# Context attention: the last norm in three pieces, with maxima between them

## The chip, the cores and the metric

The kernel runs on one core of a Trainium2 chip. The metric is the device time of one execution in microseconds (us), lower is better. Times are medians of several executions; a profile is one further execution, with every engine's instructions recorded. The engines are TensorE (PE, its weight loads shown apart as PEld), VectorE (DVE), ScalarE (ACT), GpSimd (POOL) and SyncE (SP), which here issues the DMAs.

## What is computed

Six layers follow each other on a tensor x of 8 batches, 512 tokens and 256 features; each is added to its input and normalised. The change touches the second, attention to a context:

```
wq = (q @ wq_w.T + wq_b).reshape(b, t, H, DH)          # H = 16 heads of DH = 16
wk = (k @ wk_w.T + wk_b).reshape(b, t, H, DH)
wv = (v @ wv_w.T + wv_b).reshape(b, t, H, DH)
scores = einsum('bthd,bshd->bhts', wq, wk) / sqrt(DH)
probs  = softmax(scores, axis=-1)
attn   = einsum('bhts,bshd->bthd', probs, wv).reshape(b, t, d)
...
x = _layernorm(x + (attn @ wo_w.T + wo_b))             # over the 256 features, eps 1e-5
```

Inputs and outputs are float32. The layers before it (gated linear attention) and behind it (mixture of experts, Mamba, a second attention, a gated feed-forward) are not changed.

## The kernel before

The kernel is one program in which each layer is a stage with its own buffers; a barrier stands between stages. In a stage, every engine gets its own list of instructions and runs it in order; semaphores order the engines among each other. The function of this stage is `xattn_layer`.

**Steps.** A batch has 4 quads of 4 heads, a quad 8 steps, so a batch has 32 steps and the stage 256, with a run-in and a tail. At step u, TensorE computes the scores of two heads for 128 queries, with queries as rows (`by_queries(u)`, line 734), and VectorE takes their row maxima (`maxima(u)`, line 950, one reduction of 128x1024). Sixteen steps later (`LEAD`) the same scores are made again with keys as rows and the maximum subtracted through an extra row of the operands (`by_keys(u - 16)`, line 723); ScalarE takes their exponentials (line 887), and every second step `values` multiplies these with the values (line 752). Once in 8 steps there are transposes of the maxima (line 760) and of the finished heads (line 767); VectorE then divides the heads by their sums (`normalised`, lines 959 and 965, at steps 3, 11, 19 and 27 of the 32).

**Work of a batch at fixed steps.** `starts(u, i)` is true at step i (modulo 32) for the batch that comes next, `ends(u, i)` for the one just finished. For the next batch: transposes of x at step 14, key projection at 17, query projection at 20, value projection at 28 (`token_major`, line 131, 16 matmuls of 128x256). For the finished one: transposes of its attention at 23, output projection at 25 (`OUT`; line 131 again). Within a step, TensorE's order is keys, values, queries, then transposes and projections.

**The norm.** At step 25, behind that step's maximum, VectorE waits for the output projection, adds it to x (line 1010) and runs the whole norm (`Norm.vector`): `moments` are 4 statistics (line 155), 4 aggregations (line 159) and a copy of the variance (line 169); GpSimd turns that into the reciprocal root (`Norm.gpsimd`, lines 186 and 188); `apply` waits for it and normalises x in place (line 178, 4 instructions). At step 31 SyncE waits for `x_out` and stores x.

**Regions.** All blocks of scores and projections are written to three regions of PSUM (`region`), taken in turn by `claim`. A claim makes TensorE wait until the block three claims earlier has been read: a block of keys by ScalarE's exponential, a block of queries by VectorE's maximum, the output projection by the addition, a value projection by ScalarE's copy. In the order of the claims around the norm these are: keys 26, queries 26, keys 27, queries 27, keys 28, queries 28, value projection, keys 29, queries 29, keys 30 (named by step). The output projection is claimed between queries 25 and keys 26. So keys 27 wait for the addition, keys 28 for maximum 26, the value projection for maximum 27, queries 29 for maximum 28.

The steps at which the last batches end: batch 6 ends inside the loop, but no value projection follows it, since there is no batch 8; batch 7 ends in the tail, where there are no maxima.

Of the kernel before, what the change touches and what calls it, by code (L numbers as in the profile page):

```python
# [41 lines left out]
def flat(v):  # L42
    return v.rearrange("p a n -> p (a n)")
# [7 lines left out]
def times(v, n):  # L51

    return v.unsqueeze(1).to_broadcast([v.shape[0], n, v.shape[1]])


def counter():

    return iter(range(1, 1 << 20)).__next__
# [603 lines left out]
def xattn_layer(nc, A, K, psum, x_in, x_out, weights, SLOTS):  # L662
# [3 lines left out]
    with ExitStack() as ctx:  # L666
        st = Stage(nc, ctx, "xattn", psum, K["sems"], {"short": psum[0:REGIONS], "pv": [psum[REGIONS][:, 0, :]],
                                                       "rows": [psum[REGIONS][:, 1, :]]})
        ident = K["ident"]
        wq, wk, wv, wo = (weights[n] for n in ("xwq", "xwk", "xwv", "xwo"))  # L670
        XS, RING, STEPS, LEAD = 3, 5, 2 * NT, 16
        EL, QUADS = STEPS * XQ, B * XQ
        LAST = B * EL
        xs = [st.sb(f"x{i}", [NT, D]) for i in range(XS)]
# [11 lines left out]
        norm = Norm(st, 0)  # L686
# [10 lines left out]
        def quad(u):  # L697
            return u // STEPS, u % STEPS // 2, u % 2


        def starts(u, i):
            return u // EL + 1 if u % EL == i and u // EL + 1 < B else None

        def ends(u, i):
            return u // EL - 1 if u % EL == i and 0 <= u // EL - 1 < B else None

        XT, KEYS, QUERIES, VALUES = 14, 17, 20, 28
        ATTN, OUT = 23, 25
        steps = range(-EL, LAST + EL)

        with nc.Block() as block:
# [228 lines left out]
            @block.vector  # L940
            def _(dve):
                V = nc.vector
                nth = counter()

                def maxima(u):
                    n, t, a = quad(u)
                    dve.wait_ge(*st.full(f"q{u}"))
                    if n >= 2 and u % STEPS == 0:
                        dve.wait_ge(*st.full(f"top{n - 2}"))
                    V.tensor_reduce(tops[:, n % 2, t, a::2], st.region(f"q{u}")[:], AX, ALU.max).then_inc(  # L950
                        st.emptying(f"q{u}"), 1)

                def normalised(n):
                    b, qd = divmod(n, XQ)
                    dve.wait_ge(*st.full(f"o{n}"))
                    heads = st.region(f"o{n}").rearrange("p (t h d) -> p t h d", t=NT, h=4)
                    if n:
                        dve.wait_ge(*st.emptied(f"o{n - 1}"))
                    V.reciprocal(recip[:], heads[:, :, :, 16]).then_inc(st.sem("dve_step"), 1)
                    dve.wait_ge(st.sem("dve_step"), nth())  # L960
                    if b and qd == 0:
                        dve.wait_ge(*st.full(f"attnT{b - 1}"))
                    for a in range(2):
                        at = 128 * a + 32 * qd
                        last = V.tensor_tensor(attn[:, :, at:at + 32].rearrange("p t (r d) -> p t r d", r=2),
                                               heads[:, :, 2 * a:2 * a + 2, 0:16],
                                               recip[:, :, 2 * a:2 * a + 2].unsqueeze(3).to_broadcast([P, NT, 2, 16]),
                                               ALU.mult)
                    last.then_inc(st.emptying(f"o{n}"), 1)

                def low(name, hi, lo, bias, b, count):
                    dve.wait_ge(st.sem("high"), count)
                    o = st.region(f"{name}{b}")
                    for c in range(DC):
                        last = V.scalar_tensor_tensor(lo[:, c, :], o[:, c, :], bias[:, c:c + 1],
                                                      hi[:, c, :].bitcast(F32), ALU.add, ALU.subtract)
                    last.then_inc(st.emptying(f"{name}{b}"), 1)

                V.tensor_scalar(q_bias[:], K["xwq_b"], 0.25, None, ALU.mult)
                weights.arrive(dve)  # L980
                V.tensor_scalar(wq[:], wq[:], 0.25, None, ALU.mult).then_inc(st.sem("wq_scaled"), 1)
                V.tensor_scalar(row[0:1, :], K["chunk_mask"][0:1, :], 0.0, 1.0, ALU.mult, ALU.add).then_inc(
                    st.sem("row"), 1)
                for c in range(DC):
                    last = V.tensor_scalar(v_bias[:, c, :], K["ones"][:], K["xwv_b"][:, c:c + 1], None, ALU.mult)
                last.then_inc(st.sem("v_bias"), 1)
                for va in vas:
                    V.memset(va[:, :, :, 17:32], 0.0)
                    last = V.memset(va[:, :, :, 16:17], 1.0)
                last.then_inc(st.sem("va_ones"), 1)  # L990
                for u in steps:
                    v = u - LEAD
                    if 0 <= u < LAST:
                        maxima(u)
                    if v >= 11 and v % STEPS == 3 and v // STEPS - 1 < QUADS:
                        normalised(v // STEPS - 1)
                    if (b := starts(u, KEYS)) is not None:
                        low("kp", khi, klo, K["xwk_b"], b, 2 * b + 1)
                    if (b := starts(u, QUERIES)) is not None:
                        low("qp", qhi, qlo, q_bias, b, 2 * b + 2)  # L1000
                    if starts(u, VALUES) == 0:
                        dve.wait_ge(*st.full("bias_rows"))
                        V.tensor_tensor(out_bias[:], st.region("bias_rows")[:, 0:D], K["xwo_b"], ALU.add).then_inc(
                            st.emptying("bias_rows"), 1)
                    if (b := ends(u, OUT)) is not None:
                        x = xs[b % XS]
                        dve.wait_ge(*st.full(f"out{b}"))
                        dve.wait_ge(st.sem("biased"), b + 1)
                        o = st.region(f"out{b}")
                        V.tensor_tensor(flat(x[:]), flat(x[:]), flat(o[:]), ALU.add).then_inc(st.emptying(f"out{b}"), 1)  # L1010
                        dve.wait_ge(*st.emptied(f"out{b}"))
                        norm.vector(dve, nth, x, x, "x_out")

            @block.gpsimd
            def _(pool):
                nth = counter()
                for u in steps:
                    if (b := starts(u, XT)) is not None:
                        x = xs[b % XS]
                        pool.wait_ge(*st.full(f"xT{b}"))  # L1020
                        pool.wait_ge(*st.emptied("bias_rows"))
                        nc.gpsimd.tensor_tensor(x[:], x[:], times(out_bias[:], NT), ALU.add).then_inc(
                            st.sem("biased"), 1)
                    if ends(u, OUT) is not None:
                        norm.gpsimd(pool, nth, K["neg_half"], 1e-5)
        st.zero_sems()

# [1699 lines left out]
```

## Time and profile before

| | us |
|---|---|
| median of 3 runs | 3092.56 (3082.69 to 3092.64) |
| profiled execution | 3089.96 |
| its span, first to last instruction | 3088.2 |
| TensorE busy in the span | 2559.2 (83%) |
| VectorE busy | 1638.7 (53%) |
| ScalarE busy | 1385.4 (45%) |
| GpSimd busy | 319.5 (10%) |
| mean granted TensorE clock | 0.901 of full |

Full clock is 2.4 GHz; the profile shows two levels, 1.0 and 0.5 (1.2 GHz). The context attention fills about 690 to 1356 us of the span. Additions of the output projection (line 1010) start at 843.7 us for batch 0, at 1158.09 for batch 4 and at 1345.9 for batch 7. In the bracket at the end of a row, "idle before <-releaser" is the time for which the engine stood still ahead of that instruction and what ended it.

### The profile page before, as it was taken

The numbers are of one execution on the slowest core, as the hardware profiler recorded it, in microseconds if no ns is written. First come the engines' busy times: TensorE is split into PE (matmuls) and PEld (weight loads), VectorE is DVE, ScalarE is ACT, GpSimd is POOL, SyncE is SP. The second block draws the span as 40 slices with busy tenths as digits, with TensorE's granted clock in tenths as the row PEclk, the third lists the DMA queues.
The fourth block names the chain that finished last, engine by engine and source line by source line (L and its number), as shares of the span: only waits on it lengthen the run. The fifth ranks groups of instructions, "written<-read, shape, count | busy, mean of one in ns | idle before, by whom it ended". The sixth has DMA issues, their size and how long they took to land. (4 is left out here: it accounts for less than half of the span.)

```text
span 3088.2 us, 31620 instructions
## 1 busy us (share of the span) xinstructions
PE 2559.2 (83%) x11456; PEld 1500.5 (49%) x11456; DVE 1638.7 (53%) x3416; ACT 1385.4 (45%) x1989; POOL 319.5 (10%) x299
## 2 busy tenths in 40 slices
PE   5888888857888888879998588887588888887998
PEld 3555655543333333355455355555344444444555
DVE  5665555525566666615443487878455555541222
ACT  2333333313555555532221565654277777772221
POOL 0110010000000000000166100000121111000000
PEclk8999888867999999978799799998789999998999
DMA  2000000005333333240035411111300000001000
GB/s 71 14 14 14 14 8 14 7 26 143 54 61 61 61 62 56 46 148 1 26 65 78 132 66 45 69 55 42 100 7 28 28 28 28 21 14 62 14 21 21
DMA packets 113394, 140.81 MB, mean 46 GB/s; under 512 B 22004, under 2 KB 96004, under 8 KB 113240
## 3 DMA queue, kind: packets, MB, share of 16 engines
q1 hardware_dynamic: 98888, 123.97, 14.8%
q0 software_dynamic: 11904, 14.69, 2.9%
q8 instruction: 92, 1.51, 0.2%
q14 instruction: 62, 0.51, 0.1%
q10 hardware_dynamic: 2448, 0.14, 0.1%
HBM read 77.89 MB, written 35.39 MB: 37 GB/s over the span
## 5 line engine op out<-in xcount | busy, mean ns | idle before, releaser
L950 DVE TENSOR_REDUCE xattn_tops<-region 128x2 f32<-128x1024 f32 x256 | 305.6, 1219 | 148.2 <-PE region L734 148.1
L887 ACT ACTIVATE xattn_probs<-region 128x1024 f32<-128x1024 f32 x256 | 256.2, 1022 | 154.1 <-PE region L723 153.2
L2085 PE MATMUL region<-psi_fT 128*128 128x512 f32 x512 | 247.3, 622 | 24.7 <-DVE psi_low L2361 15.2
L122 PE MATMUL region<-gla_xT,weights_even 128*128 128x512 f32 (+1 forms) x416 | 207.6, 652 | 31.3 <-ACT gla_xT L214 31.3
L723 PE MATMUL region<-xattn_qs,xattn_ks 49*128 49x512 f32 x512 | 126.6, 496 | 85.0 <-DVE xattn_tops L950 54.5
L122 PE MATMUL region<-mamba_xT,weights_odd 128*128 128x512 f32 x320 | 158.5, 644 | 3.2 <-DVE mamba_xh L1924 3.2
L2085 PEld LDWEIGHTS region<-psi_fT 128*128 128x128 f32 x512 | 93.8, 196 | 135.2 <-issue 101.9
L122 PEld LDWEIGHTS region<-gla_xT,weights_even 128*128 128x128 f32 (+1 forms) x416 | 78.0, 196 | 146.4 <-issue 110.7
L752 PE MATMUL region<-xattn_probs,xattn_va 128*32 128x512 f32 x1024 | 144.7, 633 | 1.3 <-ACT xattn_o_T L914 1.3
L131 PE MATMUL region<-weights_even,gla_work 128*128 128x256 f32 x512 | 123.5, 403 | 26.0 <-ACT gla_work L484 24.7
L734 PE MATMUL region<-xattn_ks,xattn_qs 48*128 48x512 f32 x512 | 126.5, 492 | 14.1 <-DMA xattn_ks<-xattn_khi 9.8
L2215 ACT ACTIVATE psi_wedge<-region 128x512 f32<-128x512 f32 x128 | 76.2, 595 | 117.3 <-PE region L2085 114.7
L723 PEld LDWEIGHTS region<-xattn_qs,xattn_ks 49*128 49x128 f32 x512 | 48.9, 190 | 163.5 <-DVE xattn_tops L950 95.3
L131 PEld LDWEIGHTS region<-weights_even,gla_work 128*128 128x128 f32 x512 | 103.2, 203 | 48.6 <-ACT gla_work L484 28.3
L1140 PE MATMUL region<-moe_xT,weights_even 128*128 128x512 f32 x256 | 126.7, 644 | 0.0
L734 PEld LDWEIGHTS region<-xattn_ks,xattn_qs 48*128 48x128 f32 x512 | 52.4, 201 | 135.7 <-issue 81.8
L2510 ACT ACTIVATE ffn_silu<-region 128x512 f32<-128x512 f32 x48 | 28.7, 597 | 187.3 <-PE region L2467 187.3
L471 ACT ACTIVATE gla_work<-region 128x1024 f32<-128x1024 f32 x8 | 8.2, 1024 | 220.4 <-PE region L378 220.4
L122 PEld LDWEIGHTS region<-mamba_xT,weights_odd 128*128 128x128 f32 x320 | 65.2, 209 | 85.8 <-issue 79.3
L2218 ACT ACTIVATE psi_wedge<-psi_wedge,psi_g_eps,psi_g_sq 128x512 f32<-128x512 f32 x128 | 104.1, 813 | 4.1
L2533 DVE TENSOR_TENSOR ffn_h<-ffn_silu,region 128x512 f32<-128x512 f32 x48 | 33.0, 687 | 131.1 <-ACT ffn_silu L2510 131.1
L2361 DVE CUSTOM_DVE_ANT_0 weights_even<-psi_wedge,region,psi_unsign 128x512 f32<-128x512 f32 x64 | 47.5, 746 | 86.8 <-ACT psi_wedge L2218 86.0
(501 smaller groups left out, 5226.2 us busy)
## 6 DMA issues: line engine op xcount, KB each, us to landing
weights_even<-mamba_cs SPq DMA_DIRECT2D x32, 512.0 KB, 4.6
xattn_qs<-xattn_qhi SPq DMA_DIRECT2D x128, 64.0 KB, 2.3
xattn_ks<-xattn_khi SPq DMA_DIRECT2D x128, 64.0 KB, 2.3
moe_sums<-moe_picked SPq DMA_DIRECT2D x9, 512.0 KB, 8.7
gla_x<-in_x SPq DMA_DIRECT2D x8, 512.0 KB, 3.8
x_after_gla<-gla_res SPq DMA_DIRECT2D x8, 512.0 KB, 2.9
xattn_x<-x_after_gla SPq DMA_DIRECT2D x8, 512.0 KB, 4.1
xattn_ctxT<-in_ctxT SPq DMA_DIRECT2D x8, 512.0 KB, 4.4
```

Source lines behind the costliest of these rows:

```text
L122: last = st.nc.tensor.matmul(o[0:m, i, :], w[:, c, col + i * P:col + i * P + m], rhs[:, c, :], start=c == 0, stop=c == kc - 1)
L131: last = st.nc.tensor.matmul(o[:, t * D:t * D + D], lhs[:, base + c, t * P:t * P + P], w[:, base + c, :], start=c == 0, stop=c == kc - 1)
L723: last = mm(o[:, r, :], ks[rows, ring(n), a, j * P:j * P + P], qs[rows, ring(n), a, :], start=True, stop=True)
L734: last = mm(o[:, r, :], qs[rows, ring(n), a, t * P:t * P + P], ks[rows, ring(n), a, :], start=True, stop=True)
L752: last = mm(o[32 * g:32 * g + 32, :], vas[b % 2][:, j, 2 * qd + r + 8 * a, :], probs[:, p % 3, a, r, :], start=j == 0, stop=j == NT - 1)
L887: A_(probs[:, p % 3, a, :, :], st.region(f"k{v}")[:], ACT.Exp).then_inc(st.emptying(f"k{v}"), 1)
L950: V.tensor_reduce(tops[:, n % 2, t, a::2], st.region(f"q{u}")[:], AX, ALU.max).then_inc(st.emptying(f"q{u}"), 1)
L1140: last = mm(o[:, a, :], w[:, c, (NE + i) * P:(NE + i) * P + P], xT[:, b, c, :], start=c == 0, stop=c == DC - 1)
L2085: last = mm(o[:, a, :], fT[:, h, 0, t * P:t * P + P], fT[:, h, 1 + a, :], start=True, stop=True)
L2215: A_(wedge[:, i % 2, :], st.region(f"s{b}_{i}")[:, 0, :], ACT.Relu).then_inc(st.sem("wedge_in"), 1)
L2218: A_(wedge[:, i % 2, :], wedge[:, i % 2, :], ACT.Sqrt, scale=g_sq[:], bias=g_eps[:]).then_inc(st.sem("wedge_root"), 1)
L2361: V.tensor_tensor_reduce(scores[b % 2][:, j, :], wedge[:, j % 2, :], st.region(f"s{b}_{j}")[:, 1, :], unsign[:], 1e30, ALU.add, ALU.min, l ...
```

## The change

The addition stays at step 25. The statistics move to step 26, behind that step's maximum, and the application to step 27, behind that step's maximum and the division of the heads. GpSimd's part of the norm moves to step 26 in its list. SyncE's list, the store at step 31 among it, is as it was. `moments` and `apply` are the two calls of which `Norm.vector` consists.

```diff
--- before.py
+++ after.py
@@ -1008,8 +1008,11 @@
                         dve.wait_ge(st.sem("biased"), b + 1)
                         o = st.region(f"out{b}")
                         V.tensor_tensor(flat(x[:]), flat(x[:]), flat(o[:]), ALU.add).then_inc(st.emptying(f"out{b}"), 1)
+                    if (b := ends(u, OUT + 1)) is not None:
                         dve.wait_ge(*st.emptied(f"out{b}"))
-                        norm.vector(dve, nth, x, x, "x_out")
+                        norm.moments(dve, nth, xs[b % XS])
+                    if (b := ends(u, OUT + 2)) is not None:
+                        norm.apply(dve, xs[b % XS], xs[b % XS]).then_inc(st.sem("x_out"), 1)
 
             @block.gpsimd
             def _(pool):
@@ -1021,7 +1024,7 @@
                         pool.wait_ge(*st.emptied("bias_rows"))
                         nc.gpsimd.tensor_tensor(x[:], x[:], times(out_bias[:], NT), ALU.add).then_inc(
                             st.sem("biased"), 1)
-                    if ends(u, OUT) is not None:
+                    if ends(u, OUT + 1) is not None:
                         norm.gpsimd(pool, nth, K["neg_half"], 1e-5)
         st.zero_sems()
```

## Rows read from the trace of the kernel before

**Rows 1.** The page, part 1: busy time, share of the span, instructions.
```profile
PE 2559.2 (83%) x11456; PEld 1500.5 (49%) x11456; DVE 1638.7 (53%) x3416; ACT 1385.4 (45%) x1989; POOL 319.5 (10%) x299
```

**Rows 2.** The page, part 5: line, engine, operation, count, busy and mean, idle before.
```profile
L950 DVE TENSOR_REDUCE xattn_tops<-region 128x2 f32<-128x1024 f32 x256 | 305.6, 1219 | 148.2 <-PE region L734 148.1
...
L723 PE MATMUL region<-xattn_qs,xattn_ks 49*128 49x512 f32 x512 | 126.6, 496 | 85.0 <-DVE xattn_tops L950 54.5
```

**Rows 3.** View of waits, 700 to 1376 us: who waited for whom, us, times, longest.
```profile
DVE xattn_x L178 <- POOL xattn_rstd L188: 11.8, 8, 1.5
```

**Rows 4.** Timeline of VectorE, batch 4: start us, us, line, [idle before <-releaser].
```profile
1158.09 1.22 DVE L1010 TENSOR_TENSOR xattn_x<-xattn_x,region 128x1024 f32<-128x1024 f32 x1 [2.75 <-PE region L131]
1159.34 1.41 DVE L155 BATCH_NORM_STATS2 xattn_stats<-xattn_x 128x6 f32<-128x256 f32 x4
...
1161.19 0.17 DVE L169 COPY xattn_var<-xattn_mv 128x4 f32<-128x4 f32 x1
1162.84 1.38 DVE L178 TENSOR_SCALAR xattn_x<-xattn_x,xattn_mv,xattn_rstd 128x256 f32<-128x256 f32 x4 [1.47 <-POOL xattn_rstd L188]
1164.13 2.35 DVE L950 TENSOR_REDUCE xattn_tops<-region 128x2 f32<-128x1024 f32 x2
```

**Rows 5.** Timeline of TensorE's matmuls beside it.
```profile
1158.32 0.40 PE L734 MATMUL region<-xattn_ks,xattn_qs 48*128 48x512 f32 x2
1159.36 0.50 PE L723 MATMUL region<-xattn_qs,xattn_ks 49*128 49x512 f32 x2 [0.64 <-DVE xattn_x L1010]
...
1161.22 0.66 PE L767 MATMUL region<-ident,xattn_o_T 128*128 128x128 f32 x4
1165.40 0.79 PE L723 MATMUL region<-xattn_qs,xattn_ks 49*128 49x512 f32 x2 [3.53 <-DVE xattn_tops L950]
...
1166.56 5.59 PE L131 MATMUL region<-weights_odd,xattn_ctxT 128*128 128x256 f32 x16
1172.07 0.50 PE L723 MATMUL region<-xattn_qs,xattn_ks 49*128 49x512 f32 x2
```

**Rows 6.** Windows of 1 us beside it; the third figure from the end is the clock.
```profile
1163.10:1164.10 1.00, 0.00 (x0) 0.00 (x0) 1.00 (x4) 0.00 (x0) 0.00 (x0) 0.72 0.66 103
...
1170.10:1171.10 1.00, 1.00 (x5) 0.88 (x4) 0.00 (x0) 0.00 (x0) 0.00 (x0) 0.87 0.00 0
```

**Rows 7.** Timeline of matmuls, batch 1, which has no norm at its step 25.
```profile
758.36 0.50 PE L723 MATMUL region<-xattn_qs,xattn_ks 49*128 49x512 f32 x2 [0.95 <-DVE xattn_qlo L975]
...
759.49 0.49 PE L723 MATMUL region<-xattn_qs,xattn_ks 49*128 49x512 f32 x2 [0.39 <-DVE xattn_tops L950]
...
761.58 0.63 PE L723 MATMUL region<-xattn_qs,xattn_ks 49*128 49x512 f32 x2
...
771.40 3.72 PE L131 MATMUL region<-weights_odd,xattn_ctxT 128*128 128x256 f32 x16
```

**Rows 8.** Timeline of all engines: GpSimd's bias addition beside two maxima.
```profile
1202.52 2.37 POOL L1022 TENSOR_TENSOR xattn_x<-xattn_x,xattn_out_bias 128x1024 f32<-128x1024 f32 x1 [39.72 <-PE region L114]
...
1204.33 2.35 DVE L950 TENSOR_REDUCE xattn_tops<-region 128x2 f32<-128x1024 f32 x2 [1.98 <-PE region L734]
```

**Rows 9.** Timeline, batch 6: addition, and the next blocks of line 723.
```profile
1302.78 1.22 DVE L1010 TENSOR_TENSOR xattn_x<-xattn_x,region 128x1024 f32<-128x1024 f32 x1 [2.75 <-PE region L131]
...
1310.10 0.63 PE L723 MATMUL region<-xattn_qs,xattn_ks 49*128 49x512 f32 x2 [3.53 <-DVE xattn_tops L950]
```

**Rows 10.** Windows of 1 us beside rows 7, columns as in rows 6.
```profile
759.00:760.00 1.00, 0.61 (x8) 0.28 (x10) 1.00 (x2) 0.93 (x1) 0.00 (x0) 1.00 0.39 53
760.00:761.00 1.00, 1.00 (x10) 0.09 (x10) 0.56 (x1) 0.98 (x1) 0.00 (x0) 0.88 0.65 103
```

**Rows 11.** Windows from the value projection's end to the output projection's, same columns.
```profile
775.00:843.60 68.60, 60.36 (x313) 24.55 (x312) 39.19 (x42) 38.42 (x47) 2.38 (x1) 0.90 0.29 50
...
1172.10:1236.50 64.40, 55.89 (x313) 22.50 (x312) 39.11 (x42) 38.35 (x47) 2.37 (x1) 0.97 0.26 46
```

## The prediction

> **What bounds the kernel now.** I read the page's busy times first: TensorE is busy 83% of the span and no other engine above 53% [rows 1], so what counts is where TensorE stands still. The edit touches the context-attention stage alone (about 690 to 1356 us). There the costliest groups are the row maxima on VectorE, 256 of 1219 ns, and the score matmuls of line 723, before which TensorE sat idle 85.0 us, 54.5 us of that for a maximum on VectorE [rows 2]. The view of waits has the one wait that the change is about: the last norm's application waited 11.8 us, 8 times, for GpSimd's reciprocal root [rows 3]. That sum is too small to be the point; what matters is who waits behind it.
>
> So I laid the two timelines of one batch beside each other, batch 4 of 0 to 7, whose output projection ends at 1158 us. Steps are counted modulo 32: the norm is at step 25, and TensorE's next blocks are keys and queries of steps 26 to 28, then the value projection (16 matmuls) at step 28. On VectorE: addition at 1158.09, statistics from 1159.34, their last copy ends at 1161.36, a stand until 1162.84, application until 1164.13, and only then the maxima of steps 26 and 27, together 2.35 us [rows 4]. On TensorE: step 27's work ends at 1161.88, then 3.53 us of idle, until the maximum of step 26 gives back a region; step 28's two blocks; the value projection at 1166.56, when the maximum of step 27 is ready; step 29 at 1172.07 [rows 5]. TensorE waits for VectorE here, and VectorE for the norm. The wait is on the path, since nothing else of TensorE can pass it: its queue is in order and the three regions are shared in turn.
>
> The clock falls in the same place. It goes to half its level at about 1163.5, while TensorE stands, and is back at about 1170.2 [rows 6]. So the value projection takes 5.59 us here [rows 5], where the same 16 matmuls took 3.72 us for batch 1, with no norm ahead of them [rows 7].
>
> **The change, part by part.** No instruction is added or removed: per batch the same 1 addition, 4+4+1 statistics, 2 on GpSimd and 4 applications are issued. The order on VectorE becomes addition, maximum 26, statistics, maximum 27, normalisation of the heads (step 27), application, maximum 28.
>
> *Addition.* Unmoved; it gives back the projection's region at the same moment, so keys of step 27 still start at 1159.36 [rows 5]. Zero.
>
> *Maximum 26 ahead of the statistics.* Its scores (1158.32 + 0.40) are ready before the addition ends at 1159.31 [rows 4, 5], so it runs at once, 1159.34 to about 1160.52 (half of 2.35). TensorE then doesn't wait for it at all: keys of step 28 can follow at 1161.88.
>
> *Statistics.* Their 2.02 us (1159.34 to 1161.36) [rows 4] now lie at 1160.55 to 1162.57. What is queued behind them is maximum 27, and behind that the value projection. Maximum 27 ends at 1162.6 + 1.2 = 1163.8, so the value projection starts at about 1163.88. Counted from the addition, that is 5.79 us, where it was 1166.56 - 1158.09 = 8.47: a gain of **2.68 us**. It is the stand of 1.48, the application of 1.29 and some gaps, less one start-up. TensorE itself would be there at about 1162.7 (1161.88 plus 0.8 for two blocks), so the wait is not gone: 1.2 us of it is left.
>
> *GpSimd.* Moved by one step, with nothing of its own queue between. Its 1.48 us (the stand) end at about 1164.1. The normalisation, 0.7 us after maximum 27, reaches 1164.5; the application finds the root ready with some 0.4 us to spare. The trace has no root beside a maximum. Its nearest row: a GpSimd addition of 2.37 us beside maxima of 2.35 us for two, neither longer than elsewhere [rows 8]. I take zero; the upper bound is a full maximum more, 1.2 us.
>
> *Application at step 27.* Ends at about 1165.8, maximum 28 at 1167.0. Cover: the value projection, busy to at least 1167.4; the first block that needs maximum 28 is the queries of step 29, over 1 us after that. So zero, and with GpSimd's upper bound still zero. Without the cover it would be the 1.29 us of the application. The store is issued six steps after step 25 and waits for the application only, as before.
>
> *Number of times.* Batches 0 to 5 have this form: 6 x 2.68 = 16.1 us. Batch 6 has no value projection behind it, only the 3.53 us of idle and then key blocks that need maxima 27, 28 and 29 [rows 9]; by the same arithmetic the block behind maximum 29 comes 2.7 us earlier. Batch 7 is the tail: no maxima are left, zero. Sum of the waits: **18.8 us**.
>
> *The clock.* This is the term without a row. Upper bound: with 1.2 us of idle in place of 3.53 the clock stays up and the projection takes 3.6 to 3.7 us, 6 x 1.9 = 11.4 us more. Lower bound: it falls anyway and lies on the projection, about 0.2 us each. Against the upper one speaks the trace: at 758 and 759 us TensorE was idle for only 0.95 and 0.39 us, and at about 760.4 the clock fell [rows 7, 10]. What the change leaves is 0.64 us ahead of keys of step 27 and 1.2 us ahead of the projection, close to that. In the plain loop it stays up through single waits of 0.5 to 0.9 us. I take the middle, 0.9 us each, **5.4 us**.
>
> The page "TensorE: Matmul & The Clock Gate" of the Trainium skill, section "HAM oscillation — how this bites in real kernels", ties the fall to single idle gaps longer than any that I expect here. By it the clock would stay up; the rows at 758 us speak against it as a sufficient rule. The sum by that page would be the rival "clock stays up" below.
>
> **Sum.** 16.1 + 2.7 + 5.4 = 24.2 us. The profiled execution took 3089.96 us (span 3088.2), so 3089.96 - 24.2 = **3065.8 us**. The median of the runs shown is 3092.56, 2.6 above it, their spread 10 us; I forecast by the profiled one. A gain of under 0.5% (15.5 us, about what a measurement of this kernel can tell) counts as no change.
>
> **The rivals.**
> *Clock stays up everywhere at the projection.* For it: the idle left is a third. Against it: the fall at 760.4. 18.8 + 11.4 = 30.2 us, 3059.8 us; with a low stretch less at the key projection, down to 3052. Chance 0.22.
>
> *The gain is paid back by low clock elsewhere in the batch.* Each batch becomes shorter, so the waits at the key and query projections (2.1 and 0.95 us) fall differently against the clock. What that is worth shows between the value projection and the next output projection: batch 0 to 1 took 68.6 us at a mean clock of 0.90, a later one 64.4 us at 0.97, with 313 matmuls each [rows 11]. That is 4.2 us. In three of six batches, with the projection's clock at its lower bound: 18.8 + 1.2 - 12.6 = 7.4 us, 3082.6; in one: 3074. Chance of this kind 0.21 (0.12 for a result still more than 15.5 us below).
>
> *Another wait takes over.* Maximum 27 is the new last wait, and only GpSimd's stand leaves the path, 7 x 1.48 = 10.4 us: 3079.6. For it: maximum 27 is indeed last. Against: the application has also left the way to it, by the order of the queue. The same result if the stage's pace were set by something slower than this chain, such as the stacking DMAs. Chance 0.05.
>
> *Slower.* One mechanism: the low clock as in batch 1 in all of batches 1 to 6, price 6 x 4.2 = 25.2 against 18.8 + 1.2 = 20.0: 3095. It decides from the fifth such batch on (5 x 4.2 = 21.0). Beyond 0.5% it would have to reach later stages too. Chance 0.03.
>
> *It doesn't do what it says.* The order of a queue is that of the code, so it does. Below 0.01.
>
> **How the numbers follow.** Forecast 0.48 (3060 to 3072), clock up 0.22, paid back 0.21, another wait 0.05, slower 0.03 (0.01 of it beyond 0.5%), rest 0.01. Below 3077: 0.48 + 0.22 + 0.12 = 0.82. Within 0.5%: 0.16. Above: 0.02. The range must hold 8 in 10: down to 3052 for a clock that stays up at the key projection too, up to 3079 for one or two batches paid back.
>
> **What would show it.** In the changed kernel's timeline a maximum stands between addition and statistics, and VectorE's stand for GpSimd (11.8 us) falls to the tail's 1.5. The value projection starts 5.8 us after the addition; idle ahead of line 723 for maxima falls from 54.5 by some 25 us, and some 7 us of idle appear ahead of the value projection. Its duration and the clock beside it settle the clock term: 3.7 us or 5.3. Addition to addition, 78.6 us now, becomes 74 to 75.5. Wrong would be: a projection that starts later than 5.8 us after the addition, queries of step 29 waiting for maximum 28, or a period above 76 with low clock at the key or query projection.

## The result

| | median us | runs | ratio to before (95%) |
|---|---|---|---|
| kernel before | 3092.60 (3082.69 to 3094.03) | 4 | |
| changed kernel | 3057.78 (3053.16 to 3060.05) | 4 | 0.9893 [0.9873, 0.9914] |

The change makes the kernel 1.1% faster, 34.8 us by the medians. The forecast was 3065.8 us in a range of 3052 to 3079. The profiled execution took 3060.05 us, its span is 3058.3 us, 29.9 us less than before. Seven executions of 3463 us and more, three of them of the kernel before, are left out of all medians below.

The page of the changed kernel has the two groups of [rows 2] as follows (line, engine, operation, count, busy and mean, idle before):

```profile
L950 DVE TENSOR_REDUCE xattn_tops<-region 128x2 f32<-128x1024 f32 x256 | 306.3, 1220 | 126.0 <-PE region L734 125.9
...
L723 PE MATMUL region<-xattn_qs,xattn_ks 49*128 49x512 f32 x512 | 126.4, 495 | 61.8 <-DVE xattn_tops L950 31.4
```

Idle time ahead of line 723 went from 85.0 to 61.8 us, all of it in waits for a maximum (54.5 to 31.4). The view of waits for the stage has a new wait, ahead of the value projections, and GpSimd's root is waited for only in the tail, where [rows 3] had it 8 times:

```profile
PE region L723 <- DVE xattn_tops L950: 31.4, 47, 1.2
...
PE region L131 <- DVE xattn_tops L950: 6.1, 6, 1.0
...
DVE xattn_x L178 <- POOL xattn_rstd L188: 1.5, 1, 1.5
```

Batch 4 again, VectorE's timeline, to be held against [rows 4]:

```profile
1145.62 1.22 DVE L1010 TENSOR_TENSOR xattn_x<-xattn_x,region 128x1024 f32<-128x1024 f32 x1 [2.76 <-PE region L131]
1146.76 1.22 DVE L950 TENSOR_REDUCE xattn_tops<-region 128x2 f32<-128x1024 f32 x1
1147.89 1.40 DVE L155 BATCH_NORM_STATS2 xattn_stats<-xattn_x 128x6 f32<-128x256 f32 x4
...
1149.73 0.17 DVE L169 COPY xattn_var<-xattn_mv 128x4 f32<-128x4 f32 x1
1149.81 1.22 DVE L950 TENSOR_REDUCE xattn_tops<-region 128x2 f32<-128x1024 f32 x1
...
1151.63 1.38 DVE L178 TENSOR_SCALAR xattn_x<-xattn_x,xattn_mv,xattn_rstd 128x256 f32<-128x256 f32 x4
1152.93 1.22 DVE L950 TENSOR_REDUCE xattn_tops<-region 128x2 f32<-128x1024 f32 x1
```

And TensorE's matmuls beside it, to be held against [rows 5]:

```profile
1149.67 0.39 PE L734 MATMUL region<-xattn_ks,xattn_qs 48*128 48x512 f32 x2
1151.08 3.72 PE L131 MATMUL region<-weights_odd,xattn_ctxT 128*128 128x256 f32 x16 [1.03 <-DVE xattn_tops L950]
1154.73 0.51 PE L723 MATMUL region<-xattn_qs,xattn_ks 49*128 49x512 f32 x2
...
1156.17 0.50 PE L734 MATMUL region<-xattn_ks,xattn_qs 48*128 48x512 f32 x2
```

VectorE doesn't stand still between the addition and the end of maximum 28. The value projection starts 1151.08 - 1145.62 = 5.46 us after the addition, where it was 8.47, after 1.03 us of idle, where there were 3.53 ahead of the keys of step 28; and it takes 3.72 us. Six of six are like this.

**Where the 29.9 us of the two profiles lie.** Four stretches, cut at the first key projection, the first addition and the last addition:

| stretch | before | after | |
|---|---|---|---|
| start to first key projection | 696.3 | 704.0 | +7.7 |
| to the addition of batch 0 | 147.5 | 141.0 | -6.4 |
| to the addition of batch 7 | 502.2 | 481.7 | -20.5 |
| to the end of the span | 1742.3 | 1731.6 | -10.7 |

Only in the third does an instruction stand at another place of its queue: in the fourth, batch 7's norm has no maxima beside it, and its order is as before. In the nine profiles of this study without added instructions the fourth lay between 1727.9 and 1742.3 us, and the first, which no edit touches, between 695.0 and 704.0. So a pair of profiles can't be read to better than some 14 us there, and the experiments below are read by the third stretch, from addition to addition, first and by the timed runs second.

From one addition to the next: 78.6, 78.6, 78.5, 78.5, 78.5, 66.2, 43.1 us before, 75.3, 75.3, 77.8, 72.3, 79.4, 61.3, 40.4 after. The waits (3.01) and the projection at full clock (about 1.9) make 4.92 us per batch, so one expects 73.7 in the first five. The sixth, 66.2 - 61.3 = 4.9, has just that, and the last one 2.7. The first five have in sum 11.8 us less gain than 5 x 4.92. Split by blocks, these five gained 3.1 us between key and query projection, lost 8.2 at the query projections, and lost 6.7 between them and the next addition, nearly all in the third and the fifth. That is the clock, at another place, as the timeline between the additions of batches 4 and 5 shows:

```profile
1196.97 0.50 PE L723 MATMUL region<-xattn_qs,xattn_ks 49*128 49x512 f32 x2 [2.13 <-DVE xattn_klo L975]
...
1201.23 5.73 PE L122 MATMUL region<-xattn_xT,weights_odd 128*128 128x512 f32 x8
...
1209.76 0.50 PE L723 MATMUL region<-xattn_qs,xattn_ks 49*128 49x512 f32 x2 [0.94 <-DVE xattn_qlo L975]
...
1210.89 0.50 PE L723 MATMUL region<-xattn_qs,xattn_ks 49*128 49x512 f32 x2 [0.39 <-DVE xattn_tops L950]
...
1213.12 1.97 PE L114 MATMUL region<-ident,xattn_attn 128*128 128x128 f32 x8
...
1216.93 1.93 PE L752 MATMUL region<-xattn_probs,xattn_va 128*32 128x512 f32 x8
```

The windows around the first fall (third figure from the end: granted clock) put it at about 1198.5 us, 1.5 us after TensorE resumed work behind the wait of 2.13 us:

```profile
1197.00:1198.00 1.00, 1.00 (x10) 0.31 (x10) 1.00 (x1) 0.49 (x1) 0.00 (x0) 1.00 0.00 0
1198.00:1199.00 1.00, 1.00 (x10) 0.20 (x2) 0.04 (x1) 0.53 (x1) 0.00 (x0) 0.76 0.00 0
1199.00:1200.00 1.00, 1.00 (x6) 0.71 (x4) 0.86 (x1) 0.00 (x0) 0.00 (x0) 0.50 0.00 0
```

The query projection takes 5.73 us here and 5.6 to 5.95 in three other batches; in five of the kernel before it took 3.70. The waits of 2.13, 0.94 and 0.39 us stood there before as well; only the clock answers to them otherwise. In the kernel before it was low from 1214.7 to 1218.2 us, behind the same key projection, and was back before the query projection began at 1218.96; here it is low from 1198.5 to 1205.3, mostly on the query projection. Between the additions of batches 3 and 4 it doesn't fall at all behind the same waits; that is the distance of 72.3 us, which lies below 73.7.

### The profile page after: what moved, and what is told of

It is laid out like the page before. It is cut to its first block and busy times, and to the rows that moved or that the text cites. A ratio compares the mean times of both kernels' runs of the same rounds, so it can differ in the third digit from the quotient of the medians.

```text
span 3058.3 us, 31620 instructions
## 1 busy us (share of the span) xinstructions
PE 2547.7 (83%) x11456; PEld 1497.1 (49%) x11456; DVE 1638.0 (54%) x3416; ACT 1386.3 (45%) x1989; POOL 319.9 (10%) x299
## 3 DMA queue, kind: packets, MB, share of 16 engines
q1 hardware_dynamic: 98888, 123.97, 14.9%
## 5 line engine op out<-in xcount | busy, mean ns | idle before, releaser
L723 PE MATMUL region<-xattn_qs,xattn_ks 49*128 49x512 f32 x512 | 126.4, 495 | 61.8 <-DVE xattn_tops L950 31.4
L723 PEld LDWEIGHTS region<-xattn_qs,xattn_ks 49*128 49x128 f32 x512 | 48.8, 189 | 140.5 <-DVE xattn_tops L950 71.1
```

What stands on the lines that cost most here:

```text
L723: last = mm(o[:, r, :], ks[rows, ring(n), a, j * P:j * P + P], qs[rows, ring(n), a, :], start=True, stop=True)
```

## The experiments

Beside the projection's start after the addition I give its length up to the next matmul (3.65 us at full clock), six batches each, and the stretch from first to last addition (before: 502.2, changed: 481.7).

**The changed kernel once more.**

> The changed kernel once more, in a run of its own. My theory of the 3057.8 us: the waits are worth 3.0 us in each of six batches, the value projection at full clock another 1.9 us each, and low clock at the query projection (5.6 to 5.9 us in place of 3.7 in four batches of the profile) took part of it back. If the low stretches at the query projection come from how the batch's 75 us fall against the clock, they need not lie in the same batches here: value projections again 3.72 us six times and 5.5 us after the addition, but another set of slow query projections, and 3050 to 3062 us. Rival: they belong to the code, then the same four batches are slow and the additions lie 75.3, 75.3, 77.8, 72.3, 79.4 us apart as before.

3061.45 us (3050.95 to 3066.41), ratio 0.9917 [0.9899, 0.9936]. Projections 5.47 us after the addition and 3.65 long, six times. Additions 75.3, 75.3, 79.4, 73.7, 73.7, 61.3, 39.8 us apart, stretch 478.5. The first two distances are as before, the next three aren't: two of them have the 73.7 us that the sum gives, and 9.0 us are paid back in place of 11.8. So how much is paid back isn't fixed by the code alone, and it moves a run by several us. That the first two came out alike leaves open how much of it belongs to the order. This profile was of the shortest of the five executions.

**The whole norm one step later.**

```diff
                         norm.moments(dve, nth, xs[b % XS])
-                    if (b := ends(u, OUT + 2)) is not None:
                         norm.apply(dve, xs[b % XS], xs[b % XS]).then_inc(st.sem("x_out"), 1)
```

> The addition stays at step 25, and the whole norm, statistics and application in one piece with the stand for GpSimd between, comes behind the maximum of step 26. Theory (what counts is what VectorE does ahead of the maximum of step 27, which lets the value projection start): the stand of 1.5 and the application of 1.3 us are back ahead of it, so the projection starts 8.2 to 8.5 us after the addition, as in the kernel before; TensorE's idle time moves from line 723 to the projection and gets longer in one piece (3.7 us), the clock falls there, and the time is that of the kernel before, 3085 to 3095 us. Rival (the gain is the 3.53 us in which keys of step 28 waited for the maximum of step 26): that wait is gone here too, and the time is within 5 us of the changed kernel, 3053 to 3063 us.

3099.2 us (3089.93 to 3108.74), ratio 1.0035 [1.0019, 1.0052], above the 3095 us that I had allowed for; stretch 515.8. TensorE's timeline behind the addition at 1078.88 us, and the query projection that follows:

```profile
1082.92 0.39 PE L734 MATMUL region<-xattn_ks,xattn_qs 48*128 48x512 f32 x2
1087.21 6.01 PE L131 MATMUL region<-weights_odd,xattn_ctxT 128*128 128x256 f32 x16 [3.89 <-DVE xattn_tops L950]
...
1140.23 5.09 PE L122 MATMUL region<-xattn_xT,weights_odd 128*128 128x512 f32 x8
```

The wait of line 723 is gone, as in the changed kernel, and nothing is won: the projection starts 8.33 us after the addition and takes 5.3 to 6.0 us. The theory holds for the wait and the rival falls. That it is even a little slower than before comes from elsewhere: from the addition to the end of the value projection it is 13.7 to 14.3 us, where it was 14.0 to 14.2, but in four of the first five batches the query projection takes 5.0 to 5.1 us in place of 3.6, and the way from its end to the next addition 15.6 in place of 14.0, both under low clock.

**Only the application moved.** The statistics stay at step 25, and GpSimd's part with them; against the changed kernel:

```diff
-                    if (b := ends(u, OUT + 1)) is not None:
+                    if (b := ends(u, OUT)) is not None:
                         dve.wait_ge(*st.emptied(f"out{b}"))
                         norm.moments(dve, nth, xs[b % XS])
```

> Addition and statistics both at step 25, as in the kernel before, and only the application moved behind the maximum of step 27. Theory: stand and application have left the way to the maximum of step 27, which ends as early as in the changed kernel (5.5 to 5.7 us after the addition); the keys of step 28 wait some 0.7 us for the maximum of step 26, but the value projection would have waited longer anyway. So within 4 us of the changed kernel, 3053 to 3063 us: moving the statistics is worth nothing. Rival (each of the two moves brings its part): the statistics' 2.0 us ahead of the maximum of step 26 cost about 1 to 2 us in six batches, 3064 to 3075 us.

3067.96 us (3048.31 to 3073.82), ratio 0.9932 [0.9909, 0.9955], its interval overlapping that of the changed kernel on the same chip; stretch 482.0 against 478.5 and 481.7. Idle time ahead of the projection is split in two:

```profile
1069.98 0.50 PE L723 MATMUL region<-xattn_qs,xattn_ks 49*128 49x512 f32 x2 [0.69 <-DVE xattn_tops L950]
...
1071.11 3.72 PE L131 MATMUL region<-weights_odd,xattn_ctxT 128*128 128x256 f32 x16 [0.40 <-DVE xattn_tops L950]
```

The projection starts 5.60 us after the addition instead of 5.46. By the traces the statistics' move is worth 0.14 us of wait a batch, about 1 us in all. The clock stayed up at five of six projections; one, starting at 995.66 us, took 5.33 us under low clock. The median lies 4.9 us above what I expected and in the range of the rival, whose 1 to 2 us of wait a batch the trace doesn't have. The profiled execution was the shortest of six (3048.31 us), so it can't show what the longer ones paid; whether it is more than the clock's luck stays open.

**One and two reductions more ahead of maximum 27.** Their results are used by nothing. The edit with two, a cut of it:

```diff
+        spare = st.sb("spare", [2, 2])
...
                         norm.moments(dve, nth, xs[b % XS])
+                        for i in range(2):
+                            V.tensor_reduce(spare[:, i, :], times(flat(wo[:]), 2), AX,
+                                            ALU.max)
```

> The changed kernel with one reduction of 128x1024 more on VectorE (its result is used by nothing), between the statistics of step 26 and the maximum of step 27. Theory: this is the chain that starts the value projection, so it starts 1.1 to 1.2 us later (6.6 to 6.7 us after the addition in place of 5.46), and TensorE stands 2.2 us ahead of it. 7 x 1.15 = 8 us for the wait, and for the clock, which stayed up at 1.0 us of idle and fell at 3.5 to 3.9, between nothing and 2 us in each of six batches: 3063 to 3080 us. Rival (there is slack on VectorE, it is busy only about half the time): within 3 us of the changed kernel.

> The same with two such reductions at the same place. Theory: the value projection starts 7.7 to 7.9 us after the addition, TensorE stands 3.3 us ahead of it, the clock falls there as in the kernel before, and the projection takes over 5 us: 16 us of wait and up to 12 of clock, 3075 to 3092 us. Rival: no slower than 3065 us.

One: 3066.94 us, ratio 0.9929 [0.9904, 0.9953], stretch 492.9; the projection starts 6.59 us after the addition, at full clock in four batches, while in two the projection takes 5.05 us. Two: 3098.53 us (3078.53 to 3101.93), ratio 1.0019 [0.9998, 1.0040], stretch 515.0; it starts at 7.72 and takes 5.3 to 6.5 us in all six. TensorE's rows, two of the kernel with one reduction and one of the kernel with two:

```profile
920.74 5.12 PE L131 MATMUL region<-weights_odd,xattn_ctxT 128*128 128x256 f32 x16 [2.16 <-DVE xattn_tops L951]
...
1074.90 3.72 PE L131 MATMUL region<-weights_odd,xattn_ctxT 128*128 128x256 f32 x16 [2.15 <-DVE xattn_tops L951]
```

```profile
844.34 5.41 PE L131 MATMUL region<-weights_odd,xattn_ctxT 128*128 128x256 f32 x16 [3.28 <-DVE xattn_tops L951]
```

Each reduction moves the start by 1.13 us, so this queue is the chain, without slack. The second one costs 32 us by the medians and 22 by the profiles (3063.90 to 3086.05), where the first costs 5 or 9 (over the two medians of the changed kernel). About 7 us each are the wait (6 x 1.13). Of the 22.1 us that the second adds to the stretch, 6.8 are the wait, 10.5 longer value projections, 2.5 lie in batch 6, and the rest in blocks behind the projections. For the 10 us between these two figures there is no trace. With two the median was above the 3092 us that I had allowed for.

**The same two reductions behind it.** They stand at step 27 ahead of the application.

> The same two reductions, now at step 27, behind its maximum and the division of the heads and ahead of the application. Theory (what lies behind the maximum of step 27 is covered by the value projection): the projection starts 5.46 us after the addition as in the changed kernel and takes 3.72 us; the maximum of step 28 ends some 2.3 us later, at about 10.3 us after the addition, just as TensorE reaches the queries of step 29, so nothing or up to 0.5 us is lost in each of six batches, and up to 2 us in batch 6, which has no projection: 3055 to 3066 us. Rival (any VectorE work around the norm is on the path): the same as with the two reductions ahead, 3075 us or more.

3053.31 us (3052.51 to 3057.58, three executions), ratio 0.9886 [0.9857, 0.9916]. The projection starts 5.46 us after the addition and takes 3.65 us in all six. Its end, in batch 0:

```profile
842.88 3.72 PE L131 MATMUL region<-weights_odd,xattn_ctxT 128*128 128x256 f32 x16 [1.01 <-DVE xattn_tops L951]
...
848.25 0.50 PE L735 MATMUL region<-xattn_ks,xattn_qs 48*128 48x512 f32 x2 [0.21 <-DVE xattn_tops L951]
```

2.3 us of VectorE work in each batch cost some 40 us a run on one side of maximum 27 (3098.5 against 3057.8 and 3061.5), and nothing that the timed runs show on the other; queries of step 29 wait 0.21 us, the cover's edge. The trace's stretch is 488.7 us, 7 us over the changed kernel. Of that some 2 us are waits up to the key projection (39.8 in place of 39.5 us from projection to projection), 2.2 lie in batch 6, which has no value projection as cover (42.6 in place of 40.4 us), and the rest is low clock.

**The statistics one step later still.** Statistics at step 27 with GpSimd's part, application at 28; against the changed kernel:

```diff
-                    if (b := ends(u, OUT + 1)) is not None:
+                    if (b := ends(u, OUT + 2)) is not None:
                         dve.wait_ge(*st.emptied(f"out{b}"))
                         norm.moments(dve, nth, xs[b % XS])
-                    if (b := ends(u, OUT + 2)) is not None:
+                    if (b := ends(u, OUT + 3)) is not None:
```

> Addition at step 25, statistics at step 27 behind that step's maximum and the division of the heads, application at step 28. Theory: the 1.0 us that TensorE still stands ahead of the value projection is the statistics' 2.0 us ahead of the maximum of step 27; now that maximum ends before TensorE arrives (4.4 to 4.6 us after the addition), and the projection starts at once. Queries of step 29 wait for the maximum of step 28, behind the statistics, at about 8 us after the addition; the projection covers that. 6 x 1.0 = 6 us less than the changed kernel, 3048 to 3055 us. Rival (the wait left is not the last limit, or the clock takes it back): 3055 to 3062 us, with idle time of the same size on line 723 or 734 behind the projection.

3052.99 us (3048.99 to 3061.00), ratio 0.9888 [0.9868, 0.9909], stretch 465.2. The projection follows at once:

```profile
1063.29 0.39 PE L734 MATMUL region<-xattn_ks,xattn_qs 48*128 48x512 f32 x2
1063.75 3.72 PE L131 MATMUL region<-weights_odd,xattn_ctxT 128*128 128x256 f32 x16
```

It starts at 4.52 us, 0.94 us earlier, and additions lie 71.4 us apart in three batches. In batch 6, which has no projection, the later statistics cost: 42.2 us to the next addition in place of 40.4, with waits of line 723 for maxima up from 31.4 to 33.3 us in all. So some 4 us are won in waits; the other 9 to 13 us of the stretch are low clock that this profile doesn't have. The median is 8.5 us under the changed kernel on the same chip, but the intervals overlap, so the timed runs alone don't show it.

**The projections' halves one by one.** The low clock follows upon waits behind the key and query projections; this edit shortens them.

```diff
                     for c in range(DC):
-                        last = A_(dst[:, c, :], o[:, c, :], ACT.Identity, bias=bias[:, c:c + 1])
-                    last.then_inc(st.sem("high"), 1)
+                        A_(dst[:, c, :], o[:, c, :], ACT.Identity, bias=bias[:, c:c + 1]).then_inc(st.sem("high"), 1)
...
-                    dve.wait_ge(st.sem("high"), count)
...
                     for c in range(DC):
+                        dve.wait_ge(st.sem("high"), DC * (count - 1) + c + 1)
```

> Statistics at step 27 and application at step 28 as in one_later, and at the key and query projections ScalarE reports each of its two halves by itself, so that VectorE's difference of the first half runs beside ScalarE's copy of the second. Theory: TensorE's waits behind the two projections (2.1 and 0.95 us) get shorter by up to 0.68 us each, in eight batches 7 to 10 us; and since the low clock at the query projection follows upon the wait behind the key projection, less of it is seen. 3035 to 3048 us. Rival (ScalarE and VectorE reading the same region at the same time slow each other, or the clock falls as often as before): 3047 to 3056 us.

> The changed kernel (statistics at step 26, application at 27) with the two halves of the key and query projections reported one by one. Theory: the two edits add up; the statistics' later place is worth about 6 us as between the changed kernel and one_later, so this comes to 3038 to 3050 us, and the value projection starts 5.46 us after the addition and takes 3.72 us. TensorE's waits behind the projections are those of the run with both edits. Rival (the 17 us between one_later and halves are luck of the clock in one chip's runs): 3050 to 3060 us.

> The run with both edits once more, on the same chip as halves_only: 3030 to 3042 us if its 3036 us hold, and 5 to 8 us under halves_only. Over 3046 us if they were luck of the clock.

| | median us | ratio (95%) | stretch |
|---|---|---|---|
| halves, statistics at 27 | 3036.27 | 0.9830 [0.9806, 0.9855] | 461.6 |
| the same again | 3035.27 | 0.9829 [0.9809, 0.9848] | 461.4 |
| halves, statistics at 26 | 3029.56 | 0.9819 [0.9798, 0.9840] | 461.7 |

In TensorE's waits 14.9 us behind the key projections are down to 1.6, with exponentials that now come last (9.3), and 6.6 behind the query projections to 2.6. The rows are of the first of the three:

```profile
PE region L723 <- ACT xattn_probs L887: 9.3, 6, 1.6
...
PE region L723 <- DVE xattn_qlo L974: 2.6, 7, 0.4
```

These are the fastest kernels of the study, 1.7 to 1.8% under the kernel before. The rival of slowed reads falls: ScalarE's two halves take 1.27 us and VectorE's 1.41 us as without the edit, though VectorE starts 0.72 us after ScalarE in place of 1.30. Of the 20.8 us between the profiles of the kernel before this edit (statistics at 27) and the first with it, 3.6 lie in the stretch from first to last addition, 9.3 ahead of it, where the projections of batches 0 to 2 stand and the clock, once up at 744 us, no longer falls (it fell there for 17 us in all before), and 7.0 behind it, where no edit is. But the two edits don't add up as I had written: the third kernel lies 8 us below the range that I had given, and the repeat of both edits 5.7 us over it where I had said 5 to 8 under, with intervals that overlap. The wait of 1.0 us ahead of the value projection is back in the third kernel (5.46 us after the addition) and gone in the first two (4.52), six times each, and yet the stretch is the same and the time of the third isn't longer. In its profile additions lie 71.1 to 71.2 us apart in three batches, against 71.5 to 71.6 in four of the others: with the shorter waits, the clock stays up behind the key projection in batches 0, 1 and 3 with one order and falls for 3.4 us in each of 0 to 3 with the other. Why just so I can't say.

## Why the prediction was right, and where it wasn't

- **Which wait ends last.** Right, and shown. Maximum 27 is what starts the value projection; the reductions ahead of it and behind it, and the norm in one piece, move the projection just as this has it.
- **The size of the wait.** Mis-sized by 0.33 us a batch. 3.01 us a batch, not 2.68. I let each piece start anew (1.25, 1.20 and 1.2 us); in the queue an operation of 1.22 us takes up 1.13 to 1.14, for the next one starts before its end is recorded: 1145.62, 1146.76, 1147.89. Six batches make 18.1 us, with batch 6's 2.7 in place of 18.8 now 20.8.
- **1.2 us of idle left.** 1.03, at the place named.
- **GpSimd's root.** Not waited for, as said. It ends at about 1151.35 and the application starts at 1151.63: 0.3 us to spare, where I had 0.4.
- **Cover of the application and maximum 28.** Right: queries of step 29 start at 1156.17 with no wait, and two more reductions bring just 0.21 us.
- **The clock at the projection.** Mis-sized: I took the middle, 0.9 us; it is the upper bound, 1.9 us in six of six. I had let the fall in [rows 7, 10] stand for this place. There TensorE stood for 0.95 and 0.39 us with one short block between; here it stands for 0.65 us at keys of step 27 and, after 3.2 us of work, for 1.03, with 3.7 us of matmuls behind. That this makes the difference is read from the rows, not tried. 11.5 us instead of 5.4.
- **Clock elsewhere in the batch.** This was a rival with a chance of 0.21 and a price of 4.2 us for a batch. It came true along with the other: 11.8 us were given back at and behind the query projections, and 9.0 in the repeated run. Two of the five distances, 77.8 and 79.4 us, are above the 76 that I had named as a sign of being wrong, with low clock at the query projection, so by my own sign this term was wrong. Two cases that I had set against each other both came, and nearly cancel in the profile: 20.8 + 11.5 = 32.3 us, and the stretch gained 20.5; the 11.8 are what is missing, found again block by block above.
- **The total.** 24.2 us forecast, 20.5 in the stretch, 29.9 in the pair of profiles, 34.8 by the medians, 27.5 by those of the repeated comparison (3088.93 to 3061.45). In the pair of profiles the rest over 20.5 lies in stretches whose order no edit touches and of which one varies by some 14 us between profiles. That the forecast lies between these figures is partly luck of this kind; I had only the spread of the runs in view, not that of single stretches.
- **Times of the clock's changes.** I put the fall behind [rows 7] at about 760.4 us and the return at about 1170.2; the windows of [rows 10] and [rows 6] give 760.8 and 1170.4. No sum hangs on it.
- **The page on the clock gate.** The Trainium skill's page "TensorE: Matmul & The Clock Gate", section "HAM oscillation — how this bites in real kernels", has the clock fall at idle gaps longer than any left here; ahead of the projection it did stay up. But with a gap of 2.13 to 2.16 us ahead of it, less than that page asks for, the projection ran at low clock in two of six batches, and where they differ the measurement decides.

## What to carry to other kernels

Ask of a long serial helper on one engine not how long its stalls are but which operation of that queue another engine waits for, and put everything else behind that one, up to the next block that is long enough to cover it: the same 2.3 us of VectorE work in each batch cost 40 us a run ahead of such an operation, and behind it nothing that the timed runs show. Where no such block follows, as in batch 6, the work behind costs nearly its full length (2.2 us). Where a kernel sits near a fall of TensorE's clock, cost each idle stretch twice, in waiting and in what follows it at half clock, and expect part of a gain to turn up or vanish at another place of the loop. Compare profiles by stretches that hold the edit, since those without it can differ by about half the gain.

## What the runs showed of the hardware

- **Idle ahead of 16 matmuls and the clock.** With 1.0 us of idle ahead of the value projection it ran at full clock in 24 of 24 cases (four kernels, six each), with 2.15 us in 4 of 6, with 3.3 or 3.9 in 0 of 12. With 0.7 and 0.4 us in two parts, the blocks of step 28 between them, it was 5 of 6. When it didn't, it took 5.0 to 6.5 us in place of 3.65.
- **Work without idle time doesn't bring the clock back at once.** In the changed kernel it fell at about 1212.2 us and was at half until about 1222.4, though TensorE went through scores, values, transposes and the output projection without idle time; the last rows of the timeline between the additions of batches 4 and 5 are from there (eight transposes in 1.97 us where it is 1.09 at full clock). Behind the key projection it was low for 3.4 us in some batches and for 6.8 in others, behind the same wait of 2.1 us. What decides between the two wasn't tried.
- **Records of back-to-back VectorE operations overlap by 0.08 us** (1.22 us long, 1.14 and 1.13 from start to start at 1145.62, 1146.76 and 1147.89), also a reduction and an addition that read PSUM. In a sum of a queue they count by the distance of their starts.
